# Cross-attention keys turned by VectorE from 96-column stripes instead of by TensorE, with one context buffer

## The chip, the cores and the metric

One core of one Trainium2 chip runs the whole program. The metric is device time in microseconds (us) of that core: the median of three runs for the kernel before. The profile is a separate execution of the same program. TensorE is called PE here, VectorE DVE, ScalarE ACT, GpSimd POOL and SyncE SP.

## The reference, cut to what matters

The reference is one transformer layer on x of 64 batches x 32 tokens x 512 and a context of 64 batches x 257 keys x 384, all in float32: cross-attention, self-attention and a quantized feed-forward net, each behind a LayerNorm and with a residual. Only the first part bears on the change:

```python
q = layernorm(x) @ Wq            # 16 heads of 64
k = ctx_768 @ Wk                 # 64 batches, 257 keys, 384 -> 1024
v = ctx_768 @ Wv
probs = softmax(einsum('bhsd,bhkd->bhsk', q, k) / 8)
out = einsum('bhsk,bhkd->bhsd', probs, v) @ Wo + bo
x = x + out
```

## The kernel before

The kernel never forms k or v. Since q k^T = (q Wk^T) ctx^T, the first stage (about 0 to 190 us, `project`) turns every query into a 384-wide "projected query" per head and stores it in DRAM (`qk_by_tile`). The second stage (about 190 to 1000 us) does the attention against the raw context. Self-attention and the feed-forward net follow to 1580 us; the change leaves them alone.

The second stage works in 16 tiles of 4 batches each (b = 0 to 3). Tiles 0, 1 and 15 are written out ("first", "second", "last"); tiles 2 to 14 are a loop, so all engines repeat one order of work there. Per batch, PE does this, in program order (`pe_cross_tile`):

- `pe_scores`, four row groups (rg 0 to 3) of 128 head-query rows: 9 matmuls each of projected queries (stationary) with the turned context `cT` (moving, 256 keys, in a high and a low float32r part);
- `pe_probsT` behind rg 0: 8 transposes of the previous batch's probabilities, which DVE and ACT copy out as high and low parts `pT`;
- `pe_pv`, m = 0 to 2: 6 matmuls each of `c_nat` (the context as it lies, high and low part) with `pT`. `dve_attended` copies each result out, and m = 2 uses the PSUM bank of m = 0;
- `pe_ctxT`: the next batch's 256 x 384 context is turned by six 128x128 transposes, four between m = 0 and m = 1 and two between m = 1 and m = 2. ACT copies the high part out (`act_high`, L775), DVE the low part (`dve_low`, L957);
- in batch 1 the value projection `pe_wv` (96 matmuls) between rg 2 and rg 3, in batch 3 the output projection `pe_wo` (24 matmuls) between m = 1 and m = 2.

The last of the 257 keys is handled apart: POOL subtracts the last row from the 256 others (`pool_less_last`, L1289), its scores are then zero (scores are used up to a constant per row), and its values come back as an addend `c_last` when a result is copied out. POOL also splits the context into `c_nat` high (L1304) and low (L1307) in `pool_split`, and adds a bias once per tile, in batch 1 (`pool_bias`, L1314). POOL's program order in batch b is: split(b), less_last(b+1), in batch 1 also the bias.

SP issues the DMAs in one queue. In batch b it waits for split(b) and then loads the context two batches ahead (`load_ctx(b+2)`: `c_raw`, 384 KB, and `last_row`, 192 KB), since there are two buffers each of `c_raw` and `last_row`. In batch 0 it then loads the next tile's projected queries (`load_qk`, 3 MB).

DVE's order in a batch: `row_max` of each row group, the low parts of `pT`, reciprocals, then `dve_attended` m = 0, the low parts of `cT`, two `norm` (probabilities times the inverse sum, L1181), `dve_attended` m = 1 and 2. In batch 3 it also makes the low part of the next tile's projected queries, four `dve_qk_low` of 128x1536 (L1092), each behind an `act_qk_high` on ACT.

## Time and profile before

| | |
|---|---|
| median of 3 runs | 1582.46 us (1581.96 to 1583.89) |
| span of the profiled execution | 1580.3 us |
| PE busy | 1543.1 us (98%) |
| DVE busy | 1066.2 us (67%) |
| ACT busy | 737.1 us (47%) |
| POOL busy | 371.2 us (23%) |
| period of a tile in the loop | 51.4 us (POOL's L1304 at 527.17 and at 578.54 us) |

The profile states the span from the first to the last instruction; for the profiled execution no other time is given, and the median of the runs stands 2.2 us above it. A busy share is an average over all stages. PE is busy nearly without a gap in the second stage, so work taken from it counts as long as nothing else becomes late; what becomes late is read from the timeline of one loop tile.

### The profile page before, as it was taken

The numbers are of one execution on the slowest core, as the hardware profiler recorded it, in microseconds if no ns is written. First come the engines' busy times: TensorE is split into PE (matmuls) and PEld (weight loads), VectorE is DVE, ScalarE is ACT, GpSimd is POOL, SyncE is SP. The second block draws the span as 40 slices with busy tenths as digits, with TensorE's granted clock in tenths as the row PEclk, the third lists the DMA queues.
The fourth block names the chain that finished last, engine by engine and source line by source line (L and its number), as shares of the span: only waits on it lengthen the run. The fifth ranks groups of instructions, "written<-read, shape, count | busy, mean of one in ns | idle before, by whom it ended". The sixth has DMA issues, their size and how long they took to land.

```text
span 1580.3 us, 36115 instructions
## 1 busy us (share of the span) xinstructions
PE 1543.1 (98%) x13802; PEld 1287.0 (81%) x13802; DVE 1066.2 (67%) x2306; ACT 737.1 (47%) x1596; POOL 371.2 (23%) x225
## 2 busy tenths in 40 slices
PE   7999899999999999999999999999999999998989
PEld 6888788988999899888988898878878878786544
DVE  8766677677666766776667766657555664556788
ACT  5444656455545554555545554433123222224755
POOL 1000235343444344343434344400000000000000
PEclk9999999999999999999999999999999999999999
DMA  6898864341334223431434133250311311223022
GB/s 241 318 369 345 328 238 139 125 154 57 125 138 138 90 92 138 138 133 58 141 127 153 54 128 124 81 200 22 107 63 35 115 49 42 99 84 134 1 107 107
DMA packets 78958, 210.74 MB, mean 133 GB/s; under 512 B 5712, under 2 KB 31760, under 8 KB 76048
## 3 DMA queue, kind: packets, MB, share of 16 engines
q1 hardware_dynamic: 78864, 209.39, 36.9%
q8 instruction: 71, 1.16, 0.3%
q14 instruction: 23, 0.19, 0.0%
HBM read 140.42 MB, written 68.94 MB: 132 GB/s over the span
## 4 chain that ended last, share of the span: by engine, by line
PE 75%; issue 12%; DVE 8%; ACT 4%; DMA 0%; DVEq 0%; SPq 0%; ACTq 0%; POOLq 0%; POOL 0%
PE psum_o L694 13%; PE psum_s L671 7%; PE psum_q L671 7%; PE psum_o L1488 6%; PE psum_q L1528 6%; PE psum_q L1488 6%; PE psum_t L1560 6%; PE psum_o L559 5%; PE psum_o L709 5%; DVE qk L1092 3%; PE psum_t L682 3%; PE psum_t L640 2%; PE psum_s L1515 1%; PE psum_t L591 1%; PE psum_q L591 1%
## 5 line engine op out<-in xcount | busy, mean ns | idle before, releaser
L694 PE MATMUL psum_o<-pT,c_nat 128*128 128x512 f32 x1152 | 307.3, 403 | 3.4 <-issue 2.4
L694 PEld LDWEIGHTS psum_o<-pT,c_nat 128*128 128x128 f32 x1152 | 202.7, 189 | 38.7 <-DVE pT L957 3.6
L1304 POOL TENSOR_TENSOR c_nat<-c_raw,constants 128x768 fp32r<-128x768 f32 x64 | 93.8, 1466 | 560.1 <-PE psum_o L694 445.3
L1158 DVE TENSOR_SCALAR oT<-psum_o,c_last 128x512 f32<-128x512 f32 x192 | 143.7, 748 | 65.5 <-PE psum_o L694 65.5
L671 PE MATMUL psum_s<-cT,qk 128*128 128x256 f32 (+1 forms) x1152 | 167.7, 288 | 2.3 <-DVE cT L957 0.3
L671 PEld LDWEIGHTS psum_s<-cT,qk 128*128 128x128 f32 x1152 | 151.0, 189 | 11.3 <-DVE cT L957 5.2
L671 PE MATMUL psum_q<-cT,qk 128*128 128x256 f32 (+1 forms) x1152 | 152.8, 284 | 1.0 <-DVE qk L1092 1.0
L884 ACT ACTIVATE probs<-psum_s,nmax 128x257 f32<-128x257 f32 x128 | 61.1, 477 | 197.7 <-DVE nmax L1173 197.7
L671 PEld LDWEIGHTS psum_q<-cT,qk 128*128 128x128 f32 x1152 | 143.3, 190 | 4.0 <-issue 2.6
L957 DVE TENSOR_TENSOR pT<-psum_t,pT 128x512 fp32r<-128x512 f32 x128 | 87.8, 687 | 70.9 <-ACT pT L775 70.9
L1289 POOL TENSOR_TENSOR c_raw<-c_raw,last_row 128x768 f32<-128x768 f32 x64 | 120.3, 1881 | 29.5 <-DMA last_row<-in_ctx_dram 19.1
L775 ACT ACTIVATE cT<-psum_t 128x256 fp32r<-128x256 f32 x192 | 67.1, 387 | 114.9 <-PE psum_t L640 114.8
L1307 POOL TENSOR_TENSOR c_nat<-c_raw,c_nat 128x768 fp32r<-128x768 f32 x64 | 118.3, 1849 | 5.0
L1092 DVE TENSOR_TENSOR qk<-raw,qk 128x1536 fp32r<-128x1536 f32 x62 | 107.2, 1749 | 0.0
L2318 POOL PARTITION_ALL_REDUCE tiny<-tiny x1 | 0.4, 380 | 436.8 <-DVE tiny L2234 436.8
L817 ACT ACTIVATE qk<-raw 128x1536 fp32r<-128x1536 f32 x64 | 94.5, 1512 | 0.0
L709 PE MATMUL psum_o<-oT,wv 128*64 128x128 f32 x1536 | 87.4, 274 | 0.2 <-issue 0.2
L559 PE MATMUL psum_o<-xnT,wq 128*128 128x512 f32 x372 | 87.2, 393 | 0.0
L709 PEld LDWEIGHTS psum_o<-oT,wv 128*64 128x64 f32 x1536 | 83.5, 137 | 2.4 <-issue 0.4
L1528 PE MATMUL psum_q<-w2v_high,xnT 128*128 128x512 f32 x256 | 84.7, 397 | 0.0
L559 PEld LDWEIGHTS psum_o<-xnT,wq 128*128 128x128 f32 x372 | 69.2, 188 | 16.9 <-issue 1.4
L1488 PE MATMUL psum_o<-xnT,w2k_high 128*128 128x512 f32 x256 | 82.6, 403 | 0.0
(295 smaller groups left out, 3118.2 us busy)
## 6 DMA issues: line engine op xcount, KB each, us to landing
qk_by_tile<-staged SPq DMA_DIRECT2D x32, 1536.0 KB, 10.1
raw<-qk_by_tile SPq DMA_DIRECT2D x16, 3072.0 KB, 12.3
c_raw<-in_ctx_dram SPq DMA_DIRECT2D x64, 384.0 KB, 3.3
last_row<-in_ctx_dram SPq DMA_DIRECT2D x64, 192.0 KB, 4.0
out_dram<-x_out SPq DMA_DIRECT2D x32, 256.0 KB, 2.0
x_res<-in_x_dram SPq DMA_DIRECT2D x16, 256.0 KB, 2.7
x_in<-out_dram SPq DMA_DIRECT2D x4, 1024.0 KB, 8.5
x_all<-out_dram SPq DMA_DIRECT2D x1, 4096.0 KB, 13.3
```

Of the source, the lines that this page charges most:

```text
L559: m = pe.matmul(ps[:], wq[:, part, k, j * P:(j + 1) * P], xnT[:, moving, k, :, :], start=(k, part, moving) == (0, 0, 0), stop=(k, part) == ...
L671: m = pe.matmul(ps[:, 0:keys], qk[:, part, rg, c, b, :], cT[b % 2][:, moving, c, 0:keys], start=(c, part, moving) == (0, 0, 0), stop=(c, p ...
L694: i = pe.matmul(ps[:], c_nat[(b - 1) % 2][:, part, k, m * P:(m + 1) * P], pT[:, moving, k, :], start=(k, part, moving) == (0, 0, 0), stop= ...
L709: i = pe.matmul(ps[64 * par:64 * par + 64, h4 * P:(h4 + 1) * P], wv[:, c, head * DH:(head + 1) * DH], oT[:, c, slot, :, :], start=c == 0, ...
L817: nc.scalar.activation(qk[:, 0, rg, :, :, :].rearrange("p c b (h q) -> p h (c b) q", h=4), raw[:, :, rg, :].rearrange("p h (a q) -> p h a ...
L1092: nc.vector.tensor_tensor(part[1], raw[:, :, rg, :].rearrange("p h (a q) -> p h a q", q=SQ), part[0].bitcast(F32), ALU.subtract).then_inc( ...
L1158: nc.vector.tensor_scalar(oT[:, m, :, (b - 1) % 4, :], ps[:].rearrange("p (s q) -> p s q", q=SQ), c_last[:, (b - 1) % 2, m:m + 1], None, A ...
L1289: nc.gpsimd.tensor_tensor(c_raw[i][:], c_raw[i][:], row_, ALU.subtract).then_inc(s_sub, 1)
L1307: G.tensor_tensor(c_nat[i][:, 1, :, :], c_raw[i][:], c_nat[i][:, 0, :, :].bitcast(F32), ALU.subtract).then_inc(s_nat, 1)
L1488: m = pe.matmul(ps[:], (w2_high[w], w2_low[w])[part][:, k, j * P:(j + 1) * P], xnT2[:, moving, k, :, :], start=(k, part, moving) == (0, 0, ...
L1528: m = pe.matmul(ps[:], xnT2[:, part, k, i, :], w[moving][:, k, 512 * n:512 * (n + 1)], start=(k, part, moving) == (0, 0, 0), stop=(k, part ...
L1560: m = pe.matmul(ps[:], a[:, part, k, :], w[moving][:, k, :], start=(k, part, moving) == (0, 0, 0), stop=(k, part) == (KI - 1, 1))
```

## The change

The context is loaded twice. One load is as before (`c_raw`, `last_row`), but with one buffer, one batch ahead, and it now serves `c_nat` only. The other, `load_stripes`, is four DMAs per batch: partition quadrant q (32 partitions) gets columns 96q to 96q+95 of every 32nd key, so that DVE's 32x32 block transpose (`dve_keys_turned`, one STREAM_TRANSPOSE of 768 columns) gives a turned context, with its 384 features in another order. The rows of Wk are loaded in the same order. ACT makes the high part of all three chunks in one instruction (`act_keys_high`), DVE the low part in one (`dve_keys_low`). All of `pe_ctxT` is gone. The keys are now turned without the last row subtracted, so the last key is a real column of `cT`: POOL writes it (a copy and two small TENSOR_TENSORs, `pool_last_key_taken` and `pool_last_key_split`), and all scores run over 258 columns. `dve_attended` m = 1 moves to ACT (`act_attended`).

Cut to its core (declarations, the write-up of the first tile on SP, and the removed helpers are left out):

```diff
@@ pe_scores
-            if section == "first" and rg == 0 and b < 2:
-                pe.wait_ge(s_zero, b + 1)
             if b == 0:
                 pe.wait_ge(s_qlo, 4 * t + (rg + 1))
+            if rg == 0:
+                pe.wait_ge(s_klow, 4 * t + (b + 1))
+                pe.wait_ge(s_klast, 12 * t + (3 * b + 3))
             ps, done = empty(pe, U1(("S", b, rg), t, section))
-
-            keys = SKP if section == "first" or (b, rg) == (0, 3) else 2 * P
             for c in range(KC):
-                if rg == 0:
-                    wait_chunk(pe, t, b, section, c)
                 for part, moving in PARTS:
-                    m = pe.matmul(ps[:, 0:keys], qk[:, part, rg, c, b, :], cT[b % 2][:, moving, c, 0:keys],
+                    m = pe.matmul(ps[:, 0:SKP], qk[:, part, rg, c, b, :], cT[b % 2][:, moving, c, :],
                                   start=(c, part, moving) == (0, 0, 0), stop=(c, part) == (KC - 1, 1))
@@ ACT
+        def act_keys_high(act, t, b):
+
+            act.wait_ge(s_turned, 4 * t + (b + 1))
+            nc.scalar.activation(cT[b % 2][:, 0, :, 0:2 * P], turned[b % 2], ACT.Copy).then_inc(s_khigh, 1)
+
+        def act_attended(act, t, b, m, section):
+
+            act.wait_ge(s_last, 4 * t + b)
+            ps, free = full(act, U1(("PV", b, m), t, section))
+            nc.scalar.activation(oT[:, m, :, (b - 1) % 4, :], ps[:].rearrange("p (s q) -> p s q", q=SQ), ACT.Identity,
+                                 bias=c_last[:, (b - 1) % 2, m:m + 1]).then_inc(free, 1)
@@ act_cross_tile
                 if after:
-                    ctxT(b, 0)
-                    ctxT(b, 1)
+                    act_keys_high(act, t, b + 1)
+                act_attended(act, t, b, 1, section)
                 act_last_scalars(act, t, b, section)
@@ DVE
+        def dve_keys_turned(dve, t, b):
+
+            dve.wait_ge(s_stripes, 256 * t + 64 * (b + 1))
+            nc.vector.transpose(turned[b % 2].rearrange("p c (k i) -> p k c i", i=SQ),
+                                c_stripes[:]).then_inc(s_turned, 1)
+
+        def dve_keys_low(dve, t, b):
+
+            dve.wait_ge(s_khigh, 4 * t + (b + 1))
+            nc.vector.tensor_tensor(cT[b % 2][:, 1, :, 0:2 * P], turned[b % 2],
+                                    cT[b % 2][:, 0, :, 0:2 * P].bitcast(F32), ALU.subtract).then_inc(s_klow, 1)
@@ POOL, pool_split
             pool.wait_ge(s_sub, 4 * t + (b + 1))
             G = nc.gpsimd
-            G.tensor_tensor(flat(c_nat[i][:, 0, :, :]), flat(c_raw[i][:]), zero.to_broadcast([P, 2 * DC]),
+            G.tensor_tensor(flat(c_nat[i][:, 0, :, :]), flat(c_raw[:]), zero.to_broadcast([P, 2 * DC]),
                             ALU.add).then_inc(s_chi, 1)
+            if more:
+                pool_last_key_taken(pool, t, b + 1)
             pool.wait_ge(s_chi, 4 * t + (b + 1))
-            G.tensor_tensor(c_nat[i][:, 1, :, :], c_raw[i][:], c_nat[i][:, 0, :, :].bitcast(F32),
+            G.tensor_tensor(c_nat[i][:, 1, :, :], c_raw[:], c_nat[i][:, 0, :, :].bitcast(F32),
                             ALU.subtract).then_inc(s_nat, 1)
+            if more:
+                pool_last_key_split(pool, t, b + 1)
@@ SP
+        def load_stripes(sp, batch, ahead):
+
+            keys = batch_keys(batch, ahead)
+            for q in range(4):
+                stripe = keys[:, 0:2 * P, q * STRIPE:(q + 1) * STRIPE].rearrange("a (k i) d -> i (a k) d", i=SQ)
+                sp.dma_start(c_stripes[SQ * q:SQ * (q + 1)].rearrange("p k c i -> p k (c i)"), stripe).then_inc(s_stripes, 16)
@@ sp_cross_tile
             for b in range(4):
                 if more or b < 2:
+                    sp.wait_ge(s_turned, 4 * t + (b + 2))
+                    load_stripes(sp, 4 * t, b + 2)
+                if more or b < 3:
                     sp.wait_ge(s_nat, 4 * t + (b + 1))
-                    load_ctx(sp, 4 * t, b + 2)
+                    load_ctx(sp, 4 * t, b + 1)
                 if b == 0:
                     sp.wait_ge(s_qlo, 4 * t + 4)
```

How the order of work moves, at the two places that the prediction speaks of. First DVE in batch 1 of a loop tile, from the last row maximum to the first of the next batch; `cT_90` is the turned context of batch 2, `aT_low` belongs to the value projection. Before:

```order
L1173 TENSOR_REDUCE nmax<-psum_q 128x1
L1156 REGISTER_ALU
L525 REGISTER_ALU
L1158 TENSOR_SCALAR oT<-psum_o,c_last 128x16x32
L531 REGISTER_ALU
L1177 RECIPROCAL rden<-den 128x1
L956 REGISTER_ALU
L957 TENSOR_TENSOR cT_90<-psum_t,cT_90 128x256
L956 REGISTER_ALU
L957 TENSOR_TENSOR cT_90<-psum_t,cT_90 128x256
L1180 REGISTER_ALU
L1181 TENSOR_SCALAR probs_65<-probs_65,rden 128x256
```

and of the change:

```order
L1143 TENSOR_REDUCE nmax<-psum_q 128x1
L1098 REGISTER_ALU
L1099 STREAM_TRANSPOSE turned_98<-c_stripes 128x8x3x32
L1126 REGISTER_ALU
L529 REGISTER_ALU
L1128 TENSOR_SCALAR oT<-psum_o,c_last 128x16x32
L535 REGISTER_ALU
L1147 RECIPROCAL rden<-den 128x1
L1104 REGISTER_ALU
L1105 TENSOR_TENSOR cT_90<-turned_98,cT_90 128x3x256
L1150 REGISTER_ALU
L1151 TENSOR_SCALAR probs_65<-probs_65,rden 128x256
```

The transpose stands directly behind the last row maximum and ahead of `dve_attended` m = 0, and the low part is one instruction behind it, waiting for ACT in between.

Second, SP's queue in batches 1 and 2 of a loop tile. Before:

```order
L1357 DMA c_raw_96<-in_ctx_dram 128x2x384
L1359 ISA
L1359 DMA last_row_95<-in_ctx_dram 128x384
L1434 REGISTER_ALU
L1357 ISA
L1357 DMA c_raw_92<-in_ctx_dram 128x2x384
L1359 ISA
L1359 DMA last_row_94<-in_ctx_dram 128x384
```

and of the change (the last two of four such stripe DMAs, and what stands behind them):

```order
L1350 DMA c_stripes<-in_ctx_dram 32x8x96
L1350 ISA
L1350 DMA c_stripes<-in_ctx_dram 32x8x96
L1341 DMA c_raw<-in_ctx_dram 128x2x384
L1343 ISA
L1343 DMA last_row<-in_ctx_dram 128x384
```

The load of the context as it lies now stands behind four stripe loads, and these wait for the transpose of the same batch on DVE (`s_turned`).

## Rows read from the trace of the kernel before

**Rows 1.** The page, part 1: busy time of PE and PEld over the span

```profile
PE 1543.1 (98%) x13802; PEld 1287.0 (81%) x13802; DVE 1066.2 (67%) x2306; ACT 737.1 (47%) x1596; POOL 371.2 (23%) x225
```

**Rows 2.** Timeline of PE's weight loads: first score group of three batches (start, us)

```profile
501.07 1.26 PEld L671 LDWEIGHTS psum_s<-cT,qk 128*128 128x128 f32 x9
526.62 1.25 PEld L671 LDWEIGHTS psum_s<-cT,qk 128*128 128x128 f32 x9
552.44 1.26 PEld L671 LDWEIGHTS psum_s<-cT,qk 128*128 128x128 f32 x9
```

**Rows 3.** Groups of instructions, 400 to 880 us (busy, mean ns | idle before)

```profile
L640 PEld LDWEIGHTS psum_t<-ident,c_raw 128*128 128x128 f32 x222 | 28.9, 141 | 9.8
```

**Rows 4.** Timeline of DVE: negated row maxima and one low part, four places

```profile
512.24 0.42 DVE L1173 TENSOR_REDUCE nmax<-psum_q 128x1 f32<-128x257 f32 x1
522.19 0.43 DVE L1173 TENSOR_REDUCE nmax<-psum_q 128x1 f32<-128x257 f32 x1 [0.43 <-PE psum_q L671]
532.20 0.43 DVE L1173 TENSOR_REDUCE nmax<-psum_q 128x1 f32<-128x257 f32 x1
543.94 0.43 DVE L1173 TENSOR_REDUCE nmax<-psum_s 128x1 f32<-128x257 f32 x1
546.42 0.68 DVE L957 TENSOR_TENSOR pT<-psum_t,pT 128x512 fp32r<-128x512 f32 x1
```

**Rows 5.** Groups of instructions, whole run, DVE and ACT

```profile
L1778 DVE STREAM_TRANSPOSE pT<-pr 128x512 f32<-128x512 f32 x16 | 11.4, 711 | 0.5
L1092 DVE TENSOR_TENSOR qk<-raw,qk 128x1536 fp32r<-128x1536 f32 x62 | 107.2, 1749 | 0.0
L957 DVE TENSOR_TENSOR cT<-psum_t,cT 128x256 fp32r<-128x256 f32 x192 | 74.0, 414 | 1.2 <-ACT cT L775 1.0
L1158 DVE TENSOR_SCALAR oT<-psum_o,c_last 128x512 f32<-128x512 f32 x192 | 143.7, 748 | 65.5 <-PE psum_o L694 65.5
...
L870 ACT ACTIVATE wo_high<-wo_raw 128x1024 fp32r<-128x1024 f32 x4 | 4.0, 1045 | 0.0
```

**Rows 6.** Groups of instructions, whole run, POOL

```profile
L1289 POOL TENSOR_TENSOR c_raw<-c_raw,last_row 128x768 f32<-128x768 f32 x64 | 120.3, 1881 | 29.5 <-DMA last_row<-in_ctx_dram 19.1 <-DVE qk L1092 10.4
L1307 POOL TENSOR_TENSOR c_nat<-c_raw,c_nat 128x768 fp32r<-128x768 f32 x64 | 118.3, 1849 | 5.0
L1304 POOL TENSOR_TENSOR c_nat<-c_raw,constants 128x768 fp32r<-128x768 f32 x64 | 93.8, 1466 | 560.1 <-PE psum_o L694 445.3 <-PE psum_t L546 110.1 <-DVE qk L1092 4.7
L1314 POOL TENSOR_TENSOR x_res<-x_res,bo_all 128x512 f32<-128x512 f32 x16 | 20.4, 1274 | 0.0
L1004 POOL TENSOR_SCALAR group_ln<-group_ln 128x4 f32<-128x4 f32 x1 | 0.3, 260 | 2.0 <-DVE group_ln L996 2.0
```

**Rows 7.** Timeline of SP's queue: one context load, two DMAs

```profile
505.18 0.38 SPq L1357 DMA_DIRECT2D c_raw<-in_ctx_dram  x1
505.79 0.33 SPq L1359 DMA_DIRECT2D last_row<-in_ctx_dram  x1
```

**Rows 8.** DMA view of 519 to 529 us, with that same pair alone

```profile
q1 hardware_dynamic: 416, 0.59, 18.6%
...
last_row<-in_ctx_dram SPq DMA_DIRECT2D x1, 192.0 KB, 3.1
```

**Rows 9.** Timeline of 17 to 28 us, POOL and DVE

```profile
19.91 5.69 POOL L1289 TENSOR_TENSOR c_raw<-c_raw,last_row 128x768 f32<-128x768 f32 x2 [19.05 <-DMA last_row<-in_ctx_dram]
20.59 3.31 DVE L1078 TENSOR_TENSOR wq<-wq_raw,wq 128x2048 fp32r<-128x2048 f32 x1
```

**Rows 10.** Group of instructions, whole run: DVE on 2048 columns, POOL idle

```profile
L1886 DVE TENSOR_TENSOR w2k_low<-w2k_raw,w2k_high 128x2048 fp32r<-128x2048 f32 x2 | 4.5, 2288 | 4.1 <-ACT w2k_high L1696 4.1
```

**Rows 11.** The page, part 6: load of one tile's projected queries

```profile
raw<-qk_by_tile SPq DMA_DIRECT2D x16, 3072.0 KB, 12.3
```

**Rows 12.** Timeline of the first tile: SP's queue, then PE

```profile
199.77 0.38 SPq L1357 DMA_DIRECT2D c_raw<-in_ctx_dram  x1
...
219.35 1.24 PE L671 MATMUL psum_s<-cT,qk 128*128 128x258 f32 x9
```

More of the change, by code:

```diff
@@ L51, in project_units @@
                     u += [(("XT", s + 1, i), ("s0", "s1", "t0", "t1")[i]) for i in range(4)]
-                else:
-                    u += [(("CT", "start", c), ("t0", "t1")[c]) for c in range(2)]
             for h4 in range(4):
@@ L80, in cross_units @@
             u.append((("WO",), "q1"))
-        if not (section == "last" and b == 3):
-            u += [(("CT", b, c), ("t0", "t1")[c % 2]) for c in range(3)]
     return u
@@ L726, in pe_cross_tile @@
         def pe_cross_tile(pe, t, section):
-            begun, more = section != "first", section != "last"
+            begun = section != "first"
             for b in range(4):
@@ L744, in pe_cross_tile @@
                     pe_pv(pe, t, b, 0, section)
-                if before and (more or b < 3):
-                    pe_ctxT(pe, t, b, section, (0, 1))
-                if before:
                     pe_pv(pe, t, b, 1, section)
@@ L750, in pe_cross_tile @@
                     pe_wo(pe, t, section)
-                if before and (more or b < 3):
-                    pe_ctxT(pe, t, b, section, (2,))
                 if before:
@@ L849, in act_project_all @@
                     act_group_x(act, s + 1)
-                else:
-                    for c in range(2):
-                        act_start_context(act, c)
                 for j in range(4, 8):
@@ L1249, in dve_cross_tile @@
                 if after:
-                    ctxT(b, 0)
-                    ctxT(b, 1)
+                    dve_keys_low(dve, t, b + 1)
                 norm(b, 2)
                 norm(b, 3)
-                dve_attended(dve, t, b, 1, section)
                 if qk_next:
```

195 lines of the change are left out of this document (92 added, 103 removed).

## The prediction

> **What bounds the kernel now.** I read the busy times of the page first: PE is busy 98% of the span [rows 1], so it looks as if every matmul taken away were time won. Then I read one loop tile in the timeline. Batch 1 starts on PE at 501.07, batch 3 at 526.62 and the next tile's batch 1 at 552.44 [rows 2]: 25.55 us for batches 1 and 2, 25.82 us for batch 3 and the next batch 0. The reader should see that DVE follows PE closely: the last row maximum of batch 1 starts at 512.24, that of batch 2 at 522.19, that of batch 3 at 532.20 [rows 4]. From 532.20 to 543.94, where the next tile's first row maximum starts, DVE has its longest chain (four `dve_qk_low`), and the low part of `pT` that PE's next `pe_pv` needs ends at 546.42 + 0.68 = 547.10 [rows 4]. So PE bounds most of a tile, and DVE bounds the passage from one tile to the next.
>
> **What is removed from PE.** A turned context costs six transposes, paced by their weight loads of 141 ns [rows 3]: 0.85 us per batch. 258 instead of 256 columns give back 2/256 of 36 matmuls that take 1.25 us per nine [rows 2], which is 0.04 us. Net 0.81 us per batch, 52 us for 64, if nothing else is late.
>
> **DVE and ACT.** The known transpose takes 711 ns for 512 columns [rows 5]. For 768 it lies between 0.71 and 1.07 us (by proportion); I take 1.0, near the upper end, since only a small part can be fixed. `dve_keys_low` is half of the 1.75 us instruction, 0.9. Against these 1.9 us DVE loses three low parts of 0.41 and one `dve_attended` of 0.75, together 2.0 [rows 5]. DVE's total stays. ACT's `act_keys_high` is taken as 0.85, from 1.05 us for 1024 columns [rows 5], and covered. The keys of the next batch are ready, counted from the end of the last row maximum, after 0.15 + 1.0 + 0.85 + 0.9 and some 0.3 of handovers, 3.2 us; PE meanwhile has three `pe_pv`, some 4.5 us of the 5.34 from 547.10 to 552.44 [rows 2, 4]. `dve_attended` m = 0 now stands behind the transpose and holds up m = 2 by 0 to 0.5 us a batch; it is inside the figures below.
>
> **The last key's column: the new chain.** Scores of batch b+1 now wait for a column that POOL writes behind split(b), and split(b) needs a context load that is one batch ahead only and stands on SP behind the stripes. I work it out for batches 1 and 2, counted from the start of batch 1:
>
> - last row maximum ends: 512.24 + 0.42 - 501.07 = 11.6 [rows 2, 4]; transpose 1.0: 12.6.
> - SP wakes (0.2) and issues four stripe DMAs. Two issues stand 0.6 us apart [rows 7]: 15.2 when `c_raw` is issued, 15.8 for `last_row`.
> - it lands 3.1 us later [rows 8]: 18.9.
> - POOL subtracts, 1.9: 20.8; bias 1.27: 22.05; high 1.47: 23.5; the small copy 0.2; low 1.85: 25.6; two small splits 0.5: 26.1 [rows 6]. The small operations lie between 0 and 0.26 each [rows 6]; I take 0.2 to 0.25.
>
> PE alone would want batch 3 at 25.55 - 2 x 0.81 = 23.9. It gets it at 26.1 at the earliest.
>
> **The port.** At 19.91 POOL has two subtractions that take 5.69 us together, and DVE's instruction on 2048 columns, issued in the first of them, takes 3.31 [rows 9]; elsewhere the same shape takes 2.29 [rows 10] and a subtraction 1.85. The numbers fit whole instructions in turn: DVE waits for POOL's first, POOL's second waits for DVE. The Trainium skill (SBUF — State Buffer, section "Who interferes with whom") says that a DVE instruction with two SBUF inputs contends with a GpSimd instruction that reads SBUF, and one with at most one such input does not; by this rule, with which this row agrees, the three low parts that the change removes (input from PSUM) never met POOL, and `dve_keys_low` can. Before, POOL ran early in a batch, away from `dve_qk_low`. Now it runs late, and two places collide:
>
> 1. Batch 2: POOL's high part runs 22.05 to 23.5 of the count above. The keys' low part is due at (522.19 + 0.43 - 501.07) - 0.81 + 0.15 + 1.0 + 0.85 = 22.75, so it waits for 23.5, and POOL's low part waits for it: +0.9. Batch 3 starts at 27.0 instead of 25.55: **+1.45 us**, in tiles 1 to 15: 15 x 1.45 = +21.8.
> 2. Batch 3 and the next batch 0, counted from the start of batch 3, which is 0.5 after split(2). The load for split(3) lands at 3.4; POOL works to 8.8 (1.9 + 1.47 + 0.2 + 1.85). The first `dve_qk_low` is due at 532.20 + 0.43 - 526.62 + 0.15 + 1.0 = 7.2: it waits 1.6. DVE's chain has no gap to absorb it. The next load goes out behind the stripes and lands at 7.2 + 0.2 + 2.4 + 0.6 + 3.1 = 13.5; its subtraction gets in behind `dve_keys_low` at 14.0 and holds up the rest of the chain by 1.9. The first row maximum of the next tile comes at 17.3 + 1.6 + 1.9 = 20.8 (17.3 = 543.94 - 526.62). `pT` is ready 3.15 later (547.10 - 543.94), and from there to batch 1 it took 5.34 (552.44 - 547.10); I take 4.5 without the transposes. Sum 28.45 against 25.82: **+2.6 us**, at 14 such passages: +36.8.
>
> **First and last tile.** Before, the last staged store let SP go on at 199.77 [rows 12]. Now four stripe DMAs (2.4) and then the 3 MB load (12.3 [rows 11]) go first: 214.5. The context of batch 2 is queued behind it, at about 217; subtraction, split and last key (5.9) end at 222.9, where batch 3 started at 219.35 [rows 12]: +3.6. The last tile's batch 3 keeps its gain: -0.8. Four more stripe and Wk issues at the very start I cost at nothing, since context is wanted there 100 us later; Wk in quarters could cost up to 2.
>
> **The sum**: 21.8 + 36.8 + 3.6 - 0.8 = +61.4 on the profiled span of 1580.3, so 1641.7; the median of the runs stood 2.2 above the span: **1644 us**.
>
> **Rivals.**
>
> - *Late, but no collisions.* Were POOL and DVE to pass each other without waiting, batches 1 and 2 would take 26.1 (+0.55), and the passage 17.3 + 3.15 + 4.5 = 24.95 (-0.87): 15 x 0.55 - 14 x 0.87 + 3.6 - 0.8 = -1.1, or 1581 us. Against it speaks the one clear collision [rows 9]; for it, that my offsets of POOL against DVE are good to about a microsecond.
> - *The other side: the last key is in time.* If the chain of 26.1 is 2.2 us shorter, PE is the bound again. Stripe DMAs issued at half the spacing and a quicker landing would do it. Then 15 x 1.64 + 14 x 0.87 + 0.8 = 37.6 us are won: 1545. For it speaks PE's 98% [rows 1]; it decides at 23.9 us in the count above.
> - *Small packets.* The stripes are 1024 packets of 384 bytes per batch. The pair of loads shows 384 packets of 1536 bytes (and 32 tiny ones) at 18.6% of 16 engines in 10 us [rows 8], 77 ns each. By bytes the stripes take 1.2 us of all engines, by packets 5.0. I take the low end; at the high end the load behind them lands 2.6 us later, +39, 1683. The Trainium skill (DMA: Bandwidth & Descriptors, section "Specifications") puts the least transfer at full rate at 512 bytes and says that smaller ones do a read-modify-write. No row here shows such packets in number; by an estimate from that page, at twice the bytes' time, they would still fit between the issues.
> - *POOL and DVE strictly in turn at the tile's end.* Then POOL's high and low parts also slip between the last `dve_qk_low`: 3.3 more at 14 passages, +46, 1690.
>
> **How the numbers follow.** The forecast has 0.52, with a range of its own from 1600 to 1670 (the small operations, the landing and the waits of one passage each move it by 1 us x 15). Late without collisions 0.13, split over the three outcomes since it lands on the old time; in time 0.20; small packets and strict turns together 0.15. A difference under 0.2% (3.2 us) can't be told from none. So faster 0.24, same 0.05, slower 0.71. The range reaches from 1550 to 1695: it leaves out the best of the fast case and what lies above the two slow ones.
>
> **What would show it.** Right: PE's first score group of batch 3 waits 2 to 4 us for POOL in every loop tile; `last_row` is issued some 4 us behind the transpose; POOL's instructions on 768 columns, and DVE's `dve_qk_low`, show longer means than 1.85 and 1.75; the first row maximum of a tile comes 20 us behind the start of batch 3. Wrong: waits of PE for DVE's keys (then the transpose is dearer), stripes that land 5 us or more after issue, or a tile period under 51.4 us.

## The result, and the profile after

The changed kernel takes 1662.51 us (median of four runs, 1647.31 to 1673.63); the kernel before, on the same chip, 1583.18 (1581.96 to 1584.25). The ratio is 1.0468, with a 95% interval from 1.0414 to 1.0521: **slower by 4.1 to 5.2%**; it leaves out the run of 1673.63, which counts as slow since it lies over 1.5% above the fastest. The runs of the changed kernel spread over 26 us, those of the kernel before over 2.3. The profiled execution is the fastest of the four, 1647.31 us, with a span of 1645.5 (before 1580.3), so all that is read below explains 65.2 us, and the median lies another 15 above it.

The page of the changed kernel: busy time by engine, the DMA packets, and the engines' shares of the chain that ended last.

```profile
PE 1531.4 (93%) x13413; PEld 1269.7 (77%) x13421; DVE 1141.8 (69%) x2177; ACT 768.6 (47%) x1532; POOL 483.8 (29%) x417
...
DMA packets 149501, 236.00 MB, mean 143 GB/s; under 512 B 76256, under 2 KB 102304, under 8 KB 146592
...
PE 49%; issue 33%; POOL 9%; DVE 3%; DMA 3%; ACT 1%; SPq 1%; POOLq 0%; DVEq 0%
```

PE is busy 11.7 us less than in [rows 1], although the span is 65 us longer: the saving is real, and idle time has taken its place. DVE's busy time grew by 76 us and POOL's by 113, although neither has so much more to do. The groups of instructions of the changed kernel from 200 to 1060 us show where (line, engine, operation, shapes, count, then busy us and mean ns, then idle time before and what ended it):

```profile
L1238 POOL TENSOR_TENSOR c_raw<-c_raw,last_row 128x768 f32<-128x768 f32 x62 | 136.4, 2199 | 404.6 <-DMA last_row<-in_ctx_dram 404.6
L1055 DVE TENSOR_TENSOR qk<-raw,qk 128x1536 fp32r<-128x1536 f32 x60 | 128.3, 2158 | 0.0
L1289 POOL TENSOR_TENSOR c_nat<-c_raw,c_nat 128x768 fp32r<-128x768 f32 x61 | 120.4, 1975 | 0.0
...
L1128 DVE TENSOR_SCALAR oT<-psum_o,c_last 128x512 f32<-128x512 f32 x124 | 92.0, 742 | 24.4 <-PE psum_o L668 21.5
L1151 DVE TENSOR_SCALAR probs<-probs,rden 128x256 f32<-128x256 f32 x124 | 72.9, 629 | 0.0
L1105 DVE TENSOR_TENSOR cT<-turned,cT 128x768 fp32r<-128x768 f32 x62 | 68.3, 1101 | 2.9 <-ACT cT L828 2.5
...
L1099 DVE STREAM_TRANSPOSE turned<-c_stripes 128x768 f32<-128x768 f32 x62 | 60.1, 969 | 7.6 <-DMA c_stripes<-in_ctx_dram 7.6
L828 ACT ACTIVATE cT<-turned 128x768 fp32r<-128x768 f32 x62 | 52.6, 848 | 23.3 <-DVE turned L1099 23.3
...
L1259 POOL TENSOR_TENSOR cT<-last_key,constants 128x6 fp32r<-128x6 f32 x61 | 41.2, 676 | 0.0
L1252 POOL COPY last_key<-rem_turned 128x3 f32 (+1 forms) x61 | 29.1, 477 | 0.0
```

The norms of the kernel before in the same stretch:

```profile
L1181 DVE TENSOR_SCALAR probs<-probs,rden 128x256 f32<-128x256 f32 x126 | 38.4, 348 | 0.0
```

The new parts are cheap: the turn 0.97 us, the keys' high part 0.85. What grew is what was there: the norms 0.63 us (0.35 before), the low halves of qk 2.16 (1.75), POOL's subtraction 2.20 (1.88), its low part 1.98 (1.85) [rows 5, 6]. POOL's small operations on 128 x 3 and 128 x 6 numbers (L1252, L1259) take 0.48 and 0.68 us in the mean. The addition that reads PSUM (L1128) and the turn are not longer.

The waits of the same stretch (engine, waiting line, what ended it, total us, times, longest):

```profile
PE psum_s L645 <- POOL cT L1262: 27.4, 13, 2.5
...
PE psum_o L668 <- issue: 22.4, 12, 2.5
...
PE psum_q L645 <- DVE x_out L1136: 11.8, 7, 2.2
```

The first is the last key's column, late once per tile. The other two belong to the passage from one tile to the next, and to some passages only. The timeline of the changed kernel shows three places: batch 2 of a tile (500 to 512), the passage that follows it, a long one, and the next passage (569.5 to 595.3), a short one.

```profile
500.11 1.24 PEld L645 LDWEIGHTS psum_s<-cT,qk 128*128 128x128 f32 x9
...
505.62 1.31 POOL L1298 TENSOR_TENSOR x_res<-x_res,bo_all 128x512 f32<-128x512 f32 x1
506.87 1.49 POOL L1284 TENSOR_TENSOR c_nat<-c_raw,constants 128x768 fp32r<-128x768 f32 x1
508.28 0.94 POOL L1252 COPY last_key<-rem_turned 128x3 f32 x1
509.10 2.16 DVE L1151 TENSOR_SCALAR probs<-probs,rden 128x256 f32<-128x256 f32 x2
509.18 1.92 POOL L1289 TENSOR_TENSOR c_nat<-c_raw,c_nat 128x768 fp32r<-128x768 f32 x1
511.72 1.35 PE L645 MATMUL psum_s<-cT,qk 128*128 128x258 f32 x9 [1.86 <-POOL cT L1262]
...
518.83 2.97 DVE L1055 TENSOR_TENSOR qk<-raw,qk 128x1536 fp32r<-128x1536 f32 x1
...
524.11 0.95 DVE L1105 TENSOR_TENSOR cT<-turned,cT 128x768 fp32r<-128x768 f32 x1
524.78 1.99 POOL L1238 TENSOR_TENSOR c_raw<-c_raw,last_row 128x768 f32<-128x768 f32 x1 [2.63 <-DMA last_row<-in_ctx_dram]
524.98 2.20 DVE L1151 TENSOR_SCALAR probs<-probs,rden 128x256 f32<-128x256 f32 x2
527.10 4.69 DVE L1055 TENSOR_TENSOR qk<-raw,qk 128x1536 fp32r<-128x1536 f32 x2
532.97 0.41 DVE L1143 TENSOR_REDUCE nmax<-psum_s 128x1 f32<-128x257 f32 x1
536.31 6.39 PEld L668 LDWEIGHTS psum_o<-pT,c_nat 128*128 128x128 f32 x18 [2.74 <-issue]
...
582.79 0.60 DVE L1151 TENSOR_SCALAR probs<-probs,rden 128x256 f32<-128x256 f32 x2
583.20 5.24 POOL L1238 TENSOR_TENSOR c_raw<-c_raw,last_row 128x768 f32<-128x768 f32 x1 [3.25 <-DMA last_row<-in_ctx_dram]
583.32 3.41 DVE L1055 TENSOR_TENSOR qk<-raw,qk 128x1536 fp32r<-128x1536 f32 x2
587.91 0.41 DVE L1143 TENSOR_REDUCE nmax<-psum_s 128x1 f32<-128x257 f32 x1
```

**Batch 2.** Its POOL work starts late: the high part ends at 508.36, the small copy behind it takes 0.94 us in place of 0.19, the low part ends at 511.10, the column comes behind it, and PE starts batch 3 at 511.72. Batches 1 and 2 together take 26.70 us in the mean (before 25.57).

**The passage** over batch 3 and the next batch 0 comes in two lengths: 7 of the 14 in this execution take 25.7 to 26.2 us, the other 7 from 30.4 to 32.1 (before all 25.8). In the long one, the subtraction starts before DVE's key split ends (524.78 against 525.06), and then two of the next four DVE instructions wait for one of POOL's: the first norm for the subtraction (two norms 2.20 us in place of 0.60) and the third qk low half for POOL's high part (two halves 4.69 in place of 3.41). In the short one the subtraction starts 0.3 us after the end of that split (583.20 against 581.92 + 0.95 = 582.87), in the middle of the norms; now DVE passes undisturbed, and it is POOL's subtraction that stands there for 5.24 us. The first row maximum of the next tile comes 21.3 us behind the start of batch 3 (532.97 - 511.7) in the one and 18.4 us (587.91 - 569.5) in the other. The seven long passages are not all alike. In six of them the subtraction starts between 0.35 us before and 0.17 us after the end of the key split, in the seven short ones 0.33 us or more after it; in three of the six both norms and the last qk low half wait, and the row maximum comes at 23.1 to 23.3. The seventh (tile 1) has its subtraction 1.4 us after the split, and its second and fourth qk low halves wait (2.82 and 3.39 us).

And then the clock. The windows of the changed kernel (busy us of PE, PEld, DVE, ACT and POOL, each with its count, then granted clock, DMA share, GB/s): batch 0 of the long passage, batch 0 of the short one, and the last part of the long one.

```profile
526.40:542.80 16.40, 12.54 (x64) 10.51 (x63) 12.67 (x21) 5.55 (x15) 7.21 (x6) 0.79 0.25 70
584.10:595.30 11.20, 9.60 (x63) 8.61 (x62) 9.55 (x19) 5.56 (x15) 8.06 (x6) 1.00 0.20 60
536.00:543.00 7.00, 6.68 (x19) 5.27 (x20) 4.19 (x12) 3.56 (x11) 0.00 (x0) 0.60 0.40 99
```

PE idles 2.7 us before its `pe_pv` at 536.31, and from 536 to 543 the granted clock is 0.60 in the mean, that is mostly its lower level of 1.2 GHz: 18 weight loads take 6.39 us, where 4.03 is usual. So this long passage (31.03 us) pays 1.6 (norms), 1.3 (qk) and 2.4 us (clock), which is the 5.1 us that it takes more than the mean of the short ones (25.90; the long ones' mean is 31.33), to 0.2. In all 7 long passages the granted clock of batch 0 is 0.78 to 0.80, and the 18 weight loads take 5.40 to 6.39 us: 1.4 to 2.4 us each for the clock, 13 in sum. In 4 of the 7 short ones that of batch 3 is 0.89 or 0.90; it takes 16.2 us then in place of 14.6, but batch 0 behind it 9.7 in place of 11.2, so there the lost clock is hidden behind DVE.

### The profile page after: what moved, and what is told of

The parts are those of the page before. It is cut to its first block, busy times and chain, and to the rows that moved or that the text cites. A ratio compares the mean times of both kernels' runs of the same rounds, so it can differ in the third digit from the quotient of the medians.

```text
span 1645.5 us, 35621 instructions
## 1 busy us (share of the span) xinstructions
PE 1531.4 (93%) x13413; PEld 1269.7 (77%) x13421; DVE 1141.8 (69%) x2177; ACT 768.6 (47%) x1532; POOL 483.8 (29%) x417
## 4 chain that ended last, share of the span: by engine, by line
PE 49%; issue 33%; POOL 9%; DVE 3%; DMA 3%; ACT 1%; SPq 1%; POOLq 0%; DVEq 0%
PE psum_o L1497 6%; PE psum_q L1537 5%; PE psum_q L1497 5%; PE psum_t L1569 5%; PE psum_o L563 5%; POOL c_nat L1284 4%; PE psum_q L696 4%; PE psum_o L668 3%; PE psum_s L645 2%; PE psum_q L645 2%; PE psum_s L1524 1%; PE psum_t L595 1%; PE psum_q L595 1%; DMA last_row<-in_ctx_dram 1%; PE psum_s L595 1%
## 5 line engine op out<-in xcount | busy, mean ns | idle before, releaser
L668 PE MATMUL psum_o<-pT,c_nat 128*128 128x512 f32 x1152 | 295.6, 409 | 33.6 <-issue 22.4
L668 PEld LDWEIGHTS psum_o<-pT,c_nat 128*128 128x128 f32 x1152 | 221.7, 197 | 86.4 <-issue 25.0
L1238 POOL TENSOR_TENSOR c_raw<-c_raw,last_row 128x768 f32<-128x768 f32 x64 | 140.0, 2188 | 434.1 <-DMA last_row<-in_ctx_dram 429.4
L645 PE MATMUL psum_s<-cT,qk 128*128 128x258 f32 x1152 | 170.9, 294 | 34.4 <-POOL cT L1262 27.4
L645 PE MATMUL psum_q<-cT,qk 128*128 128x258 f32 x1152 | 156.9, 287 | 14.1 <-DVE x_out L1136 11.8
L1055 DVE TENSOR_TENSOR qk<-raw,qk 128x1536 fp32r<-128x1536 f32 x62 | 131.9, 2145 | 0.2 <-ACT qk L783 0.2
L1289 POOL TENSOR_TENSOR c_nat<-c_raw,c_nat 128x768 fp32r<-128x768 f32 x64 | 126.0, 1968 | 0.2
L1128 DVE TENSOR_SCALAR oT<-psum_o,c_last 128x512 f32<-128x512 f32 x129 | 95.7, 742 | 26.5 <-PE psum_o L668 23.5
L1284 POOL TENSOR_TENSOR c_nat<-c_raw,constants 128x768 fp32r<-128x768 f32 x64 | 99.4, 1554 | 4.7 <-POOL c_raw L1238 1.4
L1497 PE MATMUL psum_q<-xnT,w2q_high 128*128 128x512 f32 x256 | 80.2, 394 | 0.0
```

The costliest lines, as they stand in the source:

```text
L645: m = pe.matmul(ps[:, 0:SKP], qk[:, part, rg, c, b, :], cT[b % 2][:, moving, c, :], start=(c, part, moving) == (0, 0, 0), stop=(c, part) = ...
L668: i = pe.matmul(ps[:], c_nat[(b - 1) % 2][:, part, k, m * P:(m + 1) * P], pT[:, moving, k, :], start=(k, part, moving) == (0, 0, 0), stop= ...
L1055: nc.vector.tensor_tensor(part[1], raw[:, :, rg, :].rearrange("p h (a q) -> p h a q", q=SQ), part[0].bitcast(F32), ALU.subtract).then_inc( ...
L1128: nc.vector.tensor_scalar(oT[:, m, :, (b - 1) % 4, :], ps[:].rearrange("p (s q) -> p s q", q=SQ), c_last[:, (b - 1) % 2, m:m + 1], None, A ...
L1238: nc.gpsimd.tensor_tensor(c_raw[:], c_raw[:], row_, ALU.subtract).then_inc(s_sub, 1)
L1284: G.tensor_tensor(flat(c_nat[i][:, 0, :, :]), flat(c_raw[:]), zero.to_broadcast([P, 2 * DC]), ALU.add).then_inc(s_chi, 1)
```

## The experiments

Theory A is that of the prediction: the context is loaded late (one buffer, behind the stripes), so the last key's column is late, and POOL's passes fall on DVE's instructions that read SBUF. Theory B puts the loss in the new way of the keys itself (small packets, the turn, the splits). The table gives for each kernel the median, its ratio to the kernel before with the 95% interval, and, from its timeline by the starts of PE's score groups, the mean length of batches 1 and 2 together (14 tiles, 2 to 15), of batch 2 alone, and of a passage, with the count of passages over 28 us among 14. The lengths come from one profiled execution each, and that of the changed kernel is 15 us under its median; so what an experiment saves by the lengths can come out some 15 us smaller than by the medians. e4 loads other keys and e7 leaves out most of POOL's passes, so the values that these two compute are wrong.

| kernel | us | ratio | batches 1+2 | batch 2 | passage | long |
|---|---|---|---|---|---|---|
| before | 1583 | 1 | 25.57 | 10.02 | 25.81 | 0 |
| changed | 1662.5 | 1.0468 (1.0414 to 1.0521) | 26.70 | 11.83 | 28.61 | 7 |
| e1_ctx_first | 1626.4 | 1.0274 (1.0257 to 1.0292) | 25.59 | 9.88 | 28.25 | 9 |
| e2_key_first | 1635.4 | 1.0347 (1.0318 to 1.0376) | 24.90 | 10.02 | 29.60 | 10 |
| e3_pool_held | 1615.9 | 1.0211 (1.0194 to 1.0228) | 26.77 | 11.91 | 26.30 | 1 |
| e4_long_packets | 1675.1 | not taken (runs 1654.8 to 1684.2) | 26.61 | 11.74 | 30.33 | 11 |
| e5_pool_at_start | 1554.3 | 0.9817 (0.9801 to 0.9833) | 24.25 | 9.38 | 24.70 | 0 |
| e6_key_first_held | 1629.4 | 1.0281 (1.0258 to 1.0303) | 24.74 | 9.88 | 28.98 | 10 |
| e7_pool_cut | 1553.8 | 0.9818 (0.9802 to 0.9835) | 24.23 | 9.37 | 24.68 | 0 |
| e8_attended_dve | 1677.8 | 1.0631 (1.0584 to 1.0679) | 26.66 | 11.79 | 30.18 | 10 |
| e9_first_tile | 1550.4 | 0.9794 (0.9781 to 0.9807) | 24.25 | 9.37 | 24.69 | 0 |
| e10_gate_only | 1590.7 | 1.0043 (1.0029 to 1.0056) | 25.58 | 10.73 | 25.73 | 1 |

### e4: long packets

```diff
-                stripe = keys[:, 0:2 * P, q * STRIPE:(q + 1) * STRIPE].rearrange("a (k i) d -> i (a k) d", i=SQ)
+                stripe = keys[:, 64 * q:64 * (q + 1), :].rearrange("a (i k) d -> i (a k d)", i=SQ)
```

> Edit: still four stripe DMAs a batch of the same 96 KB to the same partitions, but each partition gets 3072 bytes that lie together in DRAM, so the keys are wrong and the packets are few and long. Theory A (the packets' own time is hidden or small; SP's issues and the order of the loads set the landing): stripes land in about the same 2.3 us, batches 1 and 2 together 26.3 to 26.7, 1640 to 1670 us. Theory B (small packets make the landing late): the last row lands over 0.7 us earlier, batches 1 and 2 together under 26.0, under 1635 us.

Two lines of the DMA view of this run, from 200 to 1060 us:

```profile
DMA packets 45764, 121.70 MB, mean 142 GB/s; under 512 B 6614, under 2 KB 29654, under 8 KB 43829
...
c_stripes<-in_ctx_dram SPq DMA_DIRECT2D x244, 96.0 KB, 2.0
```

Of over 70,000 packets under 512 bytes in this stretch, 6,614 are left, and the stripes land 2.0 us after issue in place of 2.3. Batches 1 and 2 stay at 26.6 us, and the median (1675.1) is not lower than the changed kernel's. It lies a little above the 1670 expected: 11 passages of the profiled execution are long. The runs of the changed kernel itself spread from 1647 to 1674, probably by how many passages are long; no second execution was profiled to show it. The small packets cost nothing that shows. The trace of the changed kernel has their own time: 63,488 packets of 384 bytes take 26 ns each in the mean (packets of 1536 bytes 88 ns), so the 1024 of a batch fill 16 engines for 1.7 us.

### e7: POOL's passes cut short

```diff
+            n = 2 * DC if section == "first" else 16
-            G.tensor_tensor(flat(c_nat[i][:, 0, :, :]), flat(c_raw[:]), zero.to_broadcast([P, 2 * DC]),
+            G.tensor_tensor(flat(c_nat[i][:, 0, :, :])[:, 0:n], flat(c_raw[:])[:, 0:n], zero.to_broadcast([P, n]),
...
+                nc.gpsimd.tensor_tensor(c_raw[:, :, 0:8], c_raw[:, :, 0:8], row_[:, :, 0:8], ALU.subtract).then_inc(s_sub, 1)
```

> Edit: the changed kernel with every wait, load and order as it is, but in the tiles of the loop POOL's subtraction and two splits cover 8 of 384 columns (16 of 768), so that each lasts about 0.2 us; the context's values are then wrong. Theory A: both costs (the column 3 us later by the first split and the second, and the turns with DVE) hang on the length of POOL's passes; without it the column is ready 20.5 us after batch 1's start, against 23.9 wanted, batches 1 and 2 take 24.2 us, a passage 24.3 to 25.9: 1535 to 1560 us. Theory B (loads, packets and the turn themselves cost it): over 1620.

1553.8 us, within the range. The groups of this run (200 to 1060 us):

```profile
L1055 DVE TENSOR_TENSOR qk<-raw,qk 128x1536 fp32r<-128x1536 f32 x60 | 103.2, 1740 | 0.0
...
L1241 POOL TENSOR_TENSOR c_raw<-c_raw,last_row 128x16 f32<-128x16 f32 x62 | 46.9, 757 | 626.8 <-DMA last_row<-in_ctx_dram 626.8
L1151 DVE TENSOR_SCALAR probs<-probs,rden 128x256 f32<-128x256 f32 x126 | 38.5, 348 | 0.0
```

The subtraction still waits for the same late load behind the same stripes (626.8 us), the turn, both key splits and all packets are there, and the kernel is 1.8% faster than the one before. DVE's norms are back at 348 ns and the qk low halves at 1.74 us. The cut subtraction still takes 0.76 us in the mean where its shortest takes 0.22, since it too waits for DVE. So the whole difference of 109 us to the changed kernel hangs on how long POOL's passes last, by the column that ends late or by DVE that is held up. Theory B falls. This run alone doesn't divide the two.

### e2: the key column ahead of the splits

```diff
                 pool.wait_ge(s_klast, 12 * t + (3 * b + 3))
+                pool_last_key_taken(pool, t, b + 1)
+                pool_last_key_split(pool, t, b + 1)
             pool.wait_ge(s_sub, 4 * t + (b + 1))
```

> Edit: POOL makes the last key's column for the next batch ahead of its own two splits of the context, not between and behind them, so that the column no longer waits for the late context; all else as changed. Theory A says two things: the column's lateness is what PE waits for in batch 3's first scores (27.4 us in 13 tiles), and POOL's late splits still collide with DVE's norms and key splits. So PE's wait for the column falls below 3 us, batch 2 takes 10.3 to 11 us (now 11.6 to 12.0), the passages keep their two lengths (25.9 and 31): 1615 to 1640 us. If the column were all: 1615 and passages of 25.9. Theory B (small packets, turn): no change, 1645 to 1665.

1635.4 us. PE's wait for POOL's column is no longer among the waits, and batches 1 and 2 take 24.90 us (26.70): about 30 us over 15 tiles (404.9 - 375.2). But the passages did not keep their two lengths: they lie between 27.3 and 32.0, 29.60 in the mean, a microsecond above those of the changed kernel, and give 14 of the 30 back. The profiled span is 12.1 us shorter (1633.4 against 1645.5); that the median fell by 27, near what the column alone gives, is luck. The late column costs about 1.8 us a tile; the passages are another matter.

### e3: POOL held back in the passage

```diff
+                    if b == 3:
+                        pool.wait_ge(s_qlo, 4 * t + 8)
                     pool_less_last(pool, t, b + 1)
```

> Edit: ahead of the subtraction at the end of batch 3, POOL also waits until DVE has done its four qk low halves of the next tile; no work is taken out, POOL only starts later. Theory A (the long passages come from POOL's splits taking turns with DVE's norms and qk low halves, where the subtraction lands before the key split's end; in the short ones it is held up by DVE and comes after them): all 14 passages short, 25.8 to 26.2 us in place of 7 of 30.4 to 32.1 in the profiled execution (7 x 5.4 = 38 us), so 1605 to 1625 us, with a spread of the runs under 5 us in place of 26. Theory D (the long passages come from the landing being late, or from the clock, and POOL is only seen there): POOL later still makes all passages long, 1680 or more.

1615.9 us, 46.6 below the changed kernel's median, by a wait that was **added** (31.0 between the profiled spans, 1614.5 and 1645.5; the passages together are 32.4 us shorter). The runs lie from 1614.7 to 1619.9, a spread of 5 us in place of 26. The passages take 26.30 us in the mean; one is still at 28.25, and two others at 27.6; in these three the granted clock of batch 0 is 0.87 or 0.88, in the other eleven 1.00. Batches 1 and 2 are as before (26.77). This is what separates a late load from the turns of POOL and DVE: with POOL later still, the passages are shorter.

### e6: both together

> Edit: the edits of e2 and e3 together, on the changed kernel's order of loads. If they take away two separate costs, the savings against 1662.5 add: 27.1 (e2) and 46.6 (e3), 1589 us (1583 to 1596): about the kernel before. If both draw on one cost, 1605 to 1616.

Both edits stand in this kernel, with the changed kernel's order of loads. 1629.4, far from 1589: the savings don't add. The timeline of this run, batch 3 of one tile:

```profile
505.03 2.63 DVE L1055 TENSOR_TENSOR qk<-raw,qk 128x1536 fp32r<-128x1536 f32 x1
506.13 3.26 POOL L1289 TENSOR_TENSOR c_nat<-c_raw,c_nat 128x768 fp32r<-128x768 f32 x1
...
508.32 2.69 DVE L1055 TENSOR_TENSOR qk<-raw,qk 128x1536 fp32r<-128x1536 f32 x1
```

Batch 3 starts at 496.9 here, so POOL's low part starts 9.2 us behind it; in the changed kernel it was 6.6 (518.33 - 511.7). Part of that is the column, 0.65 us, which now goes ahead; the rest is batch 2, which is 2 us shorter, while the loads take their time as before. Now both of the first two qk low halves wait for POOL (2.63 and 2.69 us; in the changed kernel the first alone, 2.97). The hold at the batch's end comes too late for that. In e2 the passages grew in the same way: in all 14 the second qk low half waits too (2.3 to 3.0 us).

### e1: the context ahead of the stripes

```diff
+                if more or b < 3:
+                    sp.wait_ge(s_nat, 4 * t + (b + 1))
+                    load_ctx(sp, 4 * t, b + 1)
                 if more or b < 2:
                     sp.wait_ge(s_turned, 4 * t + (b + 2))
                     load_stripes(sp, 4 * t, b + 2)
-                if more or b < 3:
-                    sp.wait_ge(s_nat, 4 * t + (b + 1))
-                    load_ctx(sp, 4 * t, b + 1)
```

> Edit: in each tile of the loop SP waits for the natural copy and loads the context and its last row before it waits for the turned keys and loads the stripes. Theory A (the last key's column comes late, because the context is only loaded behind the turn and its four stripes): the subtraction runs again in the first half of a batch, PE's wait for the column (27.4 us between 200 and 1060) is gone, batches 1 and 2 together take 24.7 to 25.2 us (now 26.6), a passage over batches 3 and 0 24.5 to 26 us (now 25.8 to 32.1): 1545 to 1565 us, and faster than the kernel before. Theory B (the cost is in the way of the keys itself: small packets, the turn, the two splits of the keys): nothing of it is moved, so 1640 to 1665. Theory C (POOL and DVE collide wherever POOL's work is put): the waits move into other DVE instructions, batch 2 stays over 11 us, 1600 to 1630.

1626.4 us: 36 won, but 61 above what I expected. The late column is gone, as in e2. What theory A left out is in the timeline of this run at the end of a batch 2, which began at 482.4:

```profile
490.13 1.84 POOL L1238 TENSOR_TENSOR c_raw<-c_raw,last_row 128x768 f32<-128x768 f32 x1 [3.31 <-DMA last_row<-in_ctx_dram]
490.23 2.56 DVE L1105 TENSOR_TENSOR cT<-turned,cT 128x768 fp32r<-128x768 f32 x1
492.34 1.77 POOL L1284 TENSOR_TENSOR c_nat<-c_raw,constants 128x768 fp32r<-128x768 f32 x1 [0.37 <-PE psum_o L668]
492.71 1.82 DVE L1151 TENSOR_SCALAR probs<-probs,rden 128x256 f32<-128x256 f32 x2
493.01 1.34 PE L645 MATMUL psum_s<-cT,qk 128*128 128x258 f32 x9 [0.90 <-DVE cT L1105]
```

The subtraction, 7.7 us behind the start of batch 2 in place of 14.7, meets the key split, which takes 2.56 us in place of 0.95, and PE waits for it. "Early" was no cure: each place in the second half of a batch is bad, since there DVE splits keys, norms and, in batch 3, does its qk low halves. The first 8 us of a batch are free of these.

### e5: POOL at the start of the batch

The loads as in e1. The subtraction for batch b is no longer at the end of batch b - 1 but in `pool_split`, behind its wait for the PV:

```diff
             else:
+                pool.wait_ge(s_qlo, 4 * t + 4)
                 pool.wait_ge(filled["o1"], U1.before("o1", t, section))
...
+            if section != "first":
+                pool_less_last(pool, t, b)
             pool.wait_ge(s_sub, 4 * t + (b + 1))
...
-                if section != "last" or b < 3:
-                    pool_less_last(pool, t, b + 1)
```

> Edit: the loads in the order of e1 (context ahead of stripes), and in each tile of the loop POOL's subtraction for a batch is held until the PV of the batch before has ended (for batch 0 also until DVE's four qk low halves are done), so that its three passes over the context run together in the first 8 us of the batch, when DVE mostly reads PSUM. No work is added or taken. Theory A': what e1 still pays is where POOL's passes fall (490.13, 492.34, 518 in its trace, on DVE's key split and norms, which go from 0.95 and 0.35 us to 2.5 and 1.7). Then norms return to about 0.35 us, the key split to 0.96, the tiles take 48.5 to 49.5 us (the shortest batches seen so far, 14.83 + 9.36 + 14.63 + 9.65, sum to 48.5): 1538 to 1565 us, faster than the kernel before by 1 to 3%. Theory C (POOL's 5.7 us of passes collide wherever they are): 1600 or more. Theory B (packets, turn): 1640 or more.

1554.3 us, **faster than the kernel before by 1.7 to 2.0%**, with the same work as the changed kernel. Groups of this run (200 to 1060 us):

```profile
L1292 POOL TENSOR_TENSOR c_nat<-c_raw,c_nat 128x768 fp32r<-128x768 f32 x63 | 116.0, 1841 | 0.1
L1238 POOL TENSOR_TENSOR c_raw<-c_raw,last_row 128x768 f32<-128x768 f32 x62 | 113.9, 1837 | 384.9 <-DMA last_row<-in_ctx_dram 139.2 <-DVE qk L1055 138.6 <-PE psum_o L668 107.1
L1055 DVE TENSOR_TENSOR qk<-raw,qk 128x1536 fp32r<-128x1536 f32 x60 | 104.2, 1756 | 0.0
...
L1105 DVE TENSOR_TENSOR cT<-turned,cT 128x768 fp32r<-128x768 f32 x62 | 60.3, 973 | 4.4 <-ACT cT L828 4.0
...
L1151 DVE TENSOR_SCALAR probs<-probs,rden 128x256 f32<-128x256 f32 x126 | 38.7, 350 | 0.0
```

POOL waits 246 us in the stretch for DVE and PE by its two holds (138.6 + 107.1), and in exchange no group's mean is stretched any more on either engine: 1.84, 1.84, 1.76, 0.97 and 0.35 us. The timeline of this run shows the start of a batch 0, with POOL beside row maxima and `pT` low parts that read PSUM:

```profile
489.26 1.84 POOL L1238 TENSOR_TENSOR c_raw<-c_raw,last_row 128x768 f32<-128x768 f32 x1 [9.75 <-DVE qk L1055]
...
491.17 1.47 POOL L1287 TENSOR_TENSOR c_nat<-c_raw,constants 128x768 fp32r<-128x768 f32 x1
491.64 0.69 DVE L920 TENSOR_TENSOR pT<-psum_t,pT 128x512 fp32r<-128x512 f32 x1 [1.12 <-ACT pT L740]
```

PE's tile of 48.95 us (24.25 + 24.70, before 51.37) equals that of e7, 48.91, where POOL hardly works at all: nothing of POOL's cost in the loop is left, and PE bounds the tile again. Its share of the chain of this run is 85%.

### e10: the hold without the order of loads

> Edit: e5 without its order of loads: stripes first, context last, as in the changed kernel, and only the hold of POOL's subtraction for the end of the PV. Theory A': both halves are needed, since with this order the context lands 3 to 4 us into the next batch anyway, POOL's second split reaches the first qk low halves and the key column stays late; the hold then works in the passages only, as in e3 (1615.9): 1605 to 1625 us. If the hold alone did it: 1554 to 1570. If the hold cost more than it gives: over 1650.

This is the hold of e5 with the changed kernel's order of loads. 1590.7: better than expected, and 36 us short of e5. That much comes from the order of the loads (PE still waits 12.1 us for the late column). I had overlooked that this edit moves one more thing. In the changed kernel the bias of 1.3 us stands between the subtraction and the high part (505.62 above); with the subtraction moved into the split the bias goes ahead of it, into a time when POOL waits for the load. Batch 2 takes 10.73 us in place of 11.83, about that much. So the chain of the prediction probably had one cheap way out that neither the change nor I saw; it wasn't run alone.

### e8: the addition back on DVE

```diff
                 norm(b, 3)
+                dve_attended(dve, t, b, 1, section)
...
-                act_attended(act, t, b, 1, section)
```

> Edit: the one addition of the context's last row that the change moved from DVE to ACT goes back to DVE behind the norms, as in the kernel before. Its price is 0.75 us of DVE a batch, behind the norms and ahead of the last qk low halves: nothing where DVE has slack, and up to 0.75 us in each of the 14 passages. 1655 to 1685 us; it doesn't bring the time back in either theory. If the addition on ACT were itself a cause of the loss (ACT's exponentials held up), it would be below 1650.

1677.8 us, its interval of the ratio (1.0584 to 1.0679) above that of the changed kernel. The loss is in the passages (30.18 us, 10 of 14 long). So moving this addition to ACT was a gain of about 15 us here, by the medians.

### e9: the first tile's loads

In the first tile SP issues context 2 and stripes 3 ahead of the qk, the 2 MB of Wo (not 3) behind context 3 and stripes 4, and context 4 ahead of stripes 5; all else is e5.

> Edit: e5, and in the first tile SP issues the next tile's qk and the 3 MB of Wo later: context 2 and stripes 3 go ahead of the qk, stripes 4 ahead of Wo. In e5 PE's batches of the first tile start at 211.1, 226.0, 239.8, 251.4, 267.7, 277.0, 7.2 us later by the last than in the kernel before (195.0 to 269.8, less the 2.8 with which it begins), and PE waits there 8.0 us for DVE's addition, which stands behind the turn of stripes that took 4.9 us to issue. Theory: these waits are the loads' order; 2 to 6 us are won, 1548 to 1553 us. Rival: they come from the turn, splits and qk low halves themselves in a tile without slack: within 1 us of 1554.3.

1550.4 us (1549.1 to 1550.8), against 1551.2 to 1556.5 for e5: the fastest version, 1.9 to 2.2% under the kernel before, though its interval of the ratio overlaps that of e5 a little. Batch 1 of tile 1 starts at 245.2 us (249.3 in the changed kernel, 251.4 in e5, 243.7 before). PE's wait for the addition behind the turn fell from 8.0 to 5.2 us between 190 and 280 us, so the loads' order is part of that wait. What stays of it was not followed up.

## Why the prediction was right

The forecast was 1644 us, slower with a chance of 0.71; it came out slower, and the profiled execution at 1647.3. The median of 1662.5 is 18.5 above the forecast and inside the range: of the distance, 15 us lie between the profiled execution and the median, which the sum has no term for. By its steps, on the profiled spans (+65.2 against a forecast of +61.4):

- **PE's gain of 0.81 us per batch** was a little too high. Where nothing else is late (e5, e7), batches 1 and 2 are 1.3 us shorter than before, 0.65 per batch.
- **DVE and ACT**: turn 0.97 (1.0), low part 0.95 undisturbed (0.9), ACT 0.85 (0.85). Right. DVE's total "stays" only undisturbed: with POOL it grew by 76 us.
- **The late column** came as worked out: four stripe issues, then context and last row, the load landing in 3.6 us where 3.1 was taken; the column was ready 26.3 us after the start of batch 1 (511.59 - 485.25; forecast 26.1 without the collisions, 27.0 with them). The size was a little high: batches 1 and 2 cost 15 x 1.45 = 21.8 by the forecast, 20.8 measured (404.9 against 384.1 for 15 tiles), 4.9 of it in tile 1 and 1.13 in each of the others. e2 and e1 confirm the mechanism.
- **The passage**: +2.6 each, +36.8 in sum; measured +39.2 (400.6 against 361.4). The sum is right, its working is only half right. The first qk low half waits for POOL's low part as forecast (2.97 us in place of 1.74, 1.2 against 1.6). But the forecast had one kind of passage, with one turn of 1.9 behind the key split, and there are two. In the long one two or three of the four DVE instructions behind the split are stretched (tile 1 apart), and the clock falls: +5.5. In the short one none of them is: +0.1. That the mean of the two lies near 2.6 is luck. The step that failed is that the subtraction "gets in behind `dve_keys_low` at 14.0 and holds up the rest of the chain by 1.9": in half of the passages it held up nothing, in the others DVE lost 2.3 to 4.8 us (the row maximum at 20.8 to 23.3 in place of 18.5), by the subtraction and POOL's parts behind it.
- **The rival with strict turns** (POOL's other passes also between the last qk low halves) is thus partly true in half of the passages (the qk low halves behind the split lose 1.3 to 1.7 us there, not 3.3), though it stood apart as a case of 1690. At 5.4 us each, the 15 us between the profiled run and the median would be three more long passages; no trace of a median run was looked at, so this is only worked out.
- **The clock** was not in the prediction at all: 1.4 to 2.4 us in each of 7 long passages, 13 of the 65 us.
- **First tile**: forecast +3.6 for the start of its batch 3; that came 5.1 later than before (224.2 against 219.1), and batch 1 of tile 1 starts 5.7 later (249.3 against 243.7). Behind the last tile's batch 3 the changed kernel takes 0.4 us less than before (forecast 0.8).
- **The rival "in time"** (1545, 0.20) was the value of the change once the loads and POOL are put right: e5 and e9 reached 1554 and 1550. Its condition, a chain 2.2 us shorter, would not have been enough, as e1 shows. The turns of POOL and DVE had to go too. The rival "late, but no collisions" (1581) falls, since norms and qk low halves are stretched, and e3 shortens the passages by 32 us without making anything earlier.
- **Small packets**: e4 puts them at nothing. The two bounds were 1.2 and 5.0 us of all engines for a batch's stripes; the trace gives 1.7 (26 ns for each of 1024), near the low end that was taken, and 1.2 times the time per byte of the packets of 1536 bytes (88 ns), not twice.

Of the Trainium skill (SBUF — State Buffer, section "Who interferes with whom") the prediction used only the rule on DVE instructions with two SBUF inputs, and gave the rule for one input without its exception. The norm has one SBUF input, and it was stretched all the same (up to 2.0 us for 0.35). The exception in the same section is that a `tensor_scalar` can run in a mode that takes both port pairs and then contends too, and that the one that issues first holds them for its whole instruction. The rows agree: the norms stretch; the turn (one input) takes 0.957 to 0.983 us in all its 62 executions of the stretch in the changed kernel, in e1, e2 and e5 alike, and the addition from PSUM never more than 0.754. I had not applied that rule to the norms.

## What to carry to other kernels

A busy share doesn't tell whether two engines meet; compare the mean of each group with its mean where the other engine is idle. If they differ, look first at **when** the off-path engine does its work in the period, and hold it until the on-path engine is in its harmless stretch: e3 gained 47 us in the median by one added wait, while work moved earlier (e1) landed on other instructions. And when one buffer replaces two, walk its reload through the queue: what stands ahead of the load on that queue is now on the path.
